# A graph network kernel: the one-hot of a group made in four pieces between the additions of an earlier group

## The reference, cut to what matters

```
score = einsum(leaky_relu(xl[src] + xr[dst] + ee), att)      # edges x 4 heads
ex    = exp(score - segment_max(score, dst)[dst])
alpha = ex / segment_sum(ex, dst)[dst]
out   = segment_sum(alpha[:, :, None] * xl[src], dst)         # 6250 x 128
```

## Time and profile before

| | us |
|---|---|
| median of 3 runs (lowest, highest) | 5126.43 (5126.01, 5128.35) |
| the profiled execution: its own time | 5127.16 |
| its span, first to last instruction | 5125.2 |
| weighted pass, memset of `out` to last addition | 4330.4 to 4972.7 |

### The profile page before, as it was taken

How to read it: one execution, slowest core, us unless ns; L and a number is a source line. 1 busy time by engine, 2 the same in 40 slices (tenths; PEclk the granted TensorE clock), 3 DMA queues, 4 the chain that set the end, 5 groups by cost and what they waited for, 6 DMA issues and landing times. The chain is left out here.

```text
span 5125.2 us, 87712 instructions
## 1 busy us (share of the span) xinstructions
PE 3778.5 (74%) x18006; PEld 2578.7 (50%) x18007; DVE 3333.7 (65%) x9875; ACT 1447.6 (28%) x3473; POOL 2911.9 (57%) x2917
## 2 busy tenths in 40 slices
PE   0377777777678888599779988998988983555563
PEld 0266666666534444355446655555555552444441
DVE  5688888888788888423232244554544446788878
ACT  0255555555444444100000022222222221000012
POOL 1477777777457777777600017777777770333334
PEclk9856656565688888699989985555555555999996
DMA  5577777777433332399666636666666663655530
GB/s 103 146 251 246 251 249 252 250 250 249 160 123 97 97 97 88 77 200 201 136 193 203 203 105 173 176 179 172 178 174 176 177 158 73 163 143 142 143 102 25
DMA packets 1057653, 843.57 MB, mean 165 GB/s; under 512 B 546808, under 2 KB 952812, under 8 KB 1044022
## 3 DMA queue, kind: packets, MB, share of 16 engines
q1 hardware_dynamic: 785634, 597.46, 38.9%
q0 software_dynamic: 98096, 176.73, 13.5%
q10 hardware_dynamic: 173844, 68.53, 5.5%
HBM read 601.34 MB, written 167.28 MB: 150 GB/s over the span
## 5 line engine op out<-in xcount | busy, mean ns | idle before, releaser
L2302 POOL DMA_INDIRECT ring<-xl_rows,idx x896 | 896.4, 1000 | 788.5 <-DVE idx L2381 513.8
L413 POOL DMA_INDIRECT ringa<-x_sign_pos,idxa x880 | 865.0, 983 | 302.1 <-issue 296.0
L965 POOL DMA_INDIRECT edge_counts<-edge_cnt,places x832 | 820.7, 986 | 360.9 <-issue 272.0
L2374 PE MATMUL zps<-We,eaT 64*128 64x128 f32 x1792 | 710.8, 498 | 0.0
L2648 PE MATMUL ops<-val,hot 128*128 128x200 f32 x1792 | 369.7, 351 | 273.8 <-DVE out L2667 244.5
L2372 PE MATMUL zps<-xr,hotT 128*128 x2688 | 454.1, 301 | 149.8 <-ACT hotT L2354 76.6
L2404 DVE TENSOR_TENSOR z<-zps,ring 128x512 f32<-128x512 f32 x224 | 154.9, 691 | 607.8 <-PE zps L2374 505.5
L2374 PEld LDWEIGHTS zps<-We,eaT 64*128 64x128 f32 x1792 | 447.4, 309 | 163.6 <-issue 145.9
L2615 POOL TENSOR_TENSOR val<-rows,val 128x512 f32<-128x512 f32 x224 | 234.4, 1047 | 508.4 <-ACT val L2634 488.4
L498 PE MATMUL sela<-hota,endsa 128*128 128x128 f32 x1760 | 392.7, 393 | 132.3 <-ACT endsa L439 118.2
L2648 PEld LDWEIGHTS ops<-val,hot 128*128 128x128 f32 x1792 | 301.9, 193 | 341.5 <-DVE out L2667 307.8
(11 more groups left out here) (365 smaller groups left out, 5971.9 us busy)
## 6 DMA issues: line engine op xcount, KB each, us to landing
edge_counts<-zeroa SPq DMA_DIRECT2D x55, 1568.0 KB
matd<-edge_counts SPq DMA_DIRECT2D x12, 6272.0 KB
keyb<-edge_keys SPq DMA_DIRECT2D x50, 1216.0 KB
dstb<-dst_in_tile SPq DMA_DIRECT2D x112, 512.0 KB
xl_of_steps<-ring SPq DMA_DIRECT2D x224, 256.0 KB
rows<-xl_of_steps SPq DMA_DIRECT2D x224, 256.0 KB
reseta<-resets SPq DMA_DIRECT2D x110, 512.0 KB
dstba<-dst_in_tile_bf ACTq DMA_DIRECT2D x112, 256.0 KB
```

The costliest lines, as they stand in the source:

```text
L413: p.indirect_dma_start(out=ring[:, k, :], out_offset=None, in_=table, in_offset=bass.IndirectOffsetOnAxis(ap=idx[:, k:k + 1], axis=0)).the ...
L965: p.indirect_dma_start(out=g.M.rearrange("d s -> (d s)").unsqueeze(1), out_offset=bass.IndirectOffsetOnAxis(ap=g.place[:, c:c + 1], axis=0 ...
L2302: p.indirect_dma_start(out=ring[:, c, k, :], out_offset=None, in_=g.xl_rows[0:N, :], in_offset=bass.IndirectOffsetOnAxis(ap=idx[:, q * GS ...
L2374: ins = t.matmul(zk, eaT[:, c, k, :], g.We[:, :], start=False, stop=True)
```

## The change

The one-hot of a group is made by four `tensor_scalar` instructions of 128 columns (comparison of `iota_n` with one column of `drel`) in place of one `tensor_tensor` of 512. The first stands in front of the first addition of group G - 2, the second between the first and the second addition, and so on. The registers for the tiles of group G - 2 are loaded in front of the first piece. `s_hot` counts pieces, and TensorE waits for (G + 1) * GS of them. Each of the four additions has the wait for `s_o`, which the first alone had.

```diff
-                        wait(t, s_hot, G + 1)
+                        wait(t, s_hot, (G + 1) * GS)
...
-                def add(G, q):
+                def tiles_of(G):
                     v.load(regs, g.T[0:1, bass.ds(G * GS, GS)])
-                    T = [v.snap(r, min_val=0, max_val=NT - 1) for r in regs]
+                    return [v.snap(r, min_val=0, max_val=NT - 1) for r in regs]
+
+                def one_hot(G, c, k):
+                    v.tensor_scalar(hot[:, c, k, :], g.iota_n[:, :], g.drel[:, bass.ds(G * GS + k, 1)], None,
+                                    ALU.is_equal).then_inc(s_hot, 1)
+
+                def add(G, q, k, T):
                     wait(v, s_o, G + 1)
-                    for k in range(GS):
-
-                        wait(v, s_out, G * GS + k)
-                        to = g.out[:, bass.ds(T[k] * FX, FX)]
-                        v.tensor_tensor(to, to, ops[q % 2][k // 2][:, (k % 2) * FX:(k % 2 + 1) * FX], ALU.add
-                                        ).then_inc(s_out, 1)
+                    wait(v, s_out, G * GS + k)
+                    to = g.out[:, bass.ds(T[k] * FX, FX)]
+                    v.tensor_tensor(to, to, ops[q % 2][k // 2][:, (k % 2) * FX:(k % 2 + 1) * FX], ALU.add
+                                    ).then_inc(s_out, 1)
 
                 def body(it):
                     for q in range(NG3):
                         G, c = it * NG3 + q, q % NG
+                        adding = not (isinstance(it, int) and q < 2)
+                        if adding:
+                            T = tiles_of(G - 2)
                         wait(v, s_o, G - NG + 1)
-                        v.tensor_tensor(hot[:, c, :, :], bc_mid(g.iota_n[:, :], GS),
-                                        bc_last(g.drel[:, bass.ds(G * GS, GS)], P), ALU.is_equal).then_inc(s_hot, 1)
-                        if not (isinstance(it, int) and q < 2):
-                            add(G - 2, (q - 2) % NG)
+                        for k in range(GS):
+                            one_hot(G, c, k)
+                            if adding:
+                                add(G - 2, (q - 2) % NG, k, T)
                 turns(v, body, TURNS3)
                 for b in (2, 1):
-                    add(TURNS3 * NG3 - b, NG - b)
+                    T = tiles_of(TURNS3 * NG3 - b)
+                    for k in range(GS):
+                        add(TURNS3 * NG3 - b, NG - b, k, T)
```

## The result

The changed kernel takes 5153.04 us, median of 5 runs (5148.91 to 5157.31), beside 5128.35 for the kernel before in the same session: ratio 1.0047, 95% interval 1.0034 to 1.0059. It is slower by 25 us. The forecast was 5239, slower by 112; 5153 lies inside its range of 5121 to 5290, but the likeliest case (5197 to 5294) is refuted. Rival C, at 5155 to 5185, was nearest in number.

What follows compares the result with a forecast made beforehand. ScalarE's full queue was taken to set 2.76 us a group; with GpSimd stopping a piece each turn, 3.29. 212 groups x (3.29 - 2.76) = 112 on top of 5127 gave 5239 us, range 5121 to 5290.

Steps and rivals of the forecast that it cites:

- Rival C: VectorE's pieces are stopped now and then, two regimes alternating; 5155 to 5185 us; chance 0.13.
- the likeliest case: GpSimd's multiplication is tied to VectorE and stops a piece every turn; 5197 to 5294 us; chance 0.60.
- The pacemaker: ScalarE's full queue, with four DMA issues a group, sets 2.76 us a group in the kernel before.
- The elastic stop: On VectorE before the change, the one-hot stands still while GpSimd works; VectorE needs 2.49 of 2.76 us, so nothing is lost.
- The piece is stopped by GpSimd: A VectorE tensor_scalar waits out GpSimd's multiplication, taking 0.8 to 1.1 us and ending within 0.1 of its end.
- The pairs: On VectorE, a piece fits between dependent additions: 0.505 us a pair as before, bounds 0.48 and 0.57; added waits cost nothing.
- Where the multiplication falls: Above 2.69 us a turn, GpSimd's multiplication follows VectorE and stops a piece; the group was taken as 3.29 us.
- before piece 3 and before piece 0 no s fits: With turn 2.52 + s, s the loss per turn, no steady state has GpSimd stopping VectorE's last or first piece.
- x + 0.55: Turn's loss in us when GpSimd's multiplication starts x behind the addition in front of the stopped piece; x 0 to 0.45.
- the tied regime: GpSimd's multiplication, bound to VectorE through TensorE and ScalarE, keeps stopping piece 1 or 2; turns 3.31 or 3.05 us.
- Rival A: GpSimd's multiplication settles in the gap at VectorE's turn head, x 0.1 to 0.2, turn 2.7; 5127 us; chance 0.20.
- Rivals B and D: B: VectorE is the bound, additions' waits get covered, 5082 us, chance 0.02. D: additions leave no gap, 5203, chance 0.02.

Runs made afterwards that it cites:

- one wait: Changed kernel, but only a group's first addition waits for TensorE (s_o); 5127.10 us, ratio 0.9998, on the main chip.
- waits swapped: Changed kernel with an addition's two waits written in the other order, s_out first, then s_o; 5129.79 us, ratio 1.0007.
- one wait, SyncE issues 2: Changed kernel with s_o waited for at the first addition only, and two of a group's four feature DMAs issued by SyncE instead of ScalarE; 5213.53 us, ratio 1.0164.
- before, SyncE issues 2: Kernel before, with two of a group's four feature DMAs issued by SyncE instead of ScalarE; 6546.07 us on another chip, ratio 0.9971.

## Why the prediction was wrong, and where it was right

**The pacemaker: right.** With two DMAs fewer in ScalarE's queue the kernel before runs 2.610 for 2.762. **The elastic stop: right.** Taken away, it changes no time. **The piece is stopped by GpSimd: right**: every stopped piece of the changed kernel ends 0.080 to 0.084 behind the end of the multiplication, within the 0.1 predicted.

**The pairs: 0.505 is right for the pieces, wrong for the waits.** The forecast took 0.20 for a piece and fitted it under the 0.50; it takes 0.28, and the pair is 0.505 all the same, as the next addition starts some 0.06 before the piece is over (4603.10 + 0.28 against 4603.32). The other half of the step failed. The forecast said that the added waits "are for things long done. Nothing." They are what makes the change slower at all. Alone they cost 0.07 in three pairs of six groups in eight, and that counts because of what it uses up. VectorE's undisturbed turn is 0.98 (piece at 0.77 behind the last addition, addition 0.21 behind it) + 3 x 0.505 = 2.49, with 0.20 in hand under ScalarE's 2.69. With three pairs of 0.575 it is 2.70: nothing in hand. (The forecast's upper bound for a pair was 0.57, but for a longer piece and not for the waits; that the two numbers agree is chance.) In the runs without the costly order ScalarE never waits (0.001 a group); in the changed kernel it waits 0.079.

**Where the multiplication falls: the step of the 112 us that failed.** The sum priced a group at 3.29 for 2.76, a loss of 0.53; measured is 2.850, a loss of 0.088. The forecast held that once a turn is over 2.69, a regime with T of 3.05 to 3.31 holds itself, with piece 1 or 2 stopped, and that "before piece 3 and before piece 0 no s fits". Measured over groups 56 to 200: in the changed kernel 84 last pieces and 12 first ones are stopped, none of the second or third. The error is in the price of a stop of the last piece, x + 0.55. It counts the piece's wait but not what the queue does during it: the load of T and its register operations run, and the next first piece starts at 0.27 for 0.77. Half a microsecond comes back, so by the same sum a stop of the last piece costs x + 0.05. The eight turns of a loop pass (last addition to last addition, the median of each over groups 56 to 200) are 2.68, 2.95, 2.65, 3.02, 2.68, 2.32, 2.71 and 3.63 us, a mean of 2.83, and not 3.29. I had used the same overlap for the kernel before (the load runs "behind hot's back") and did not carry it over. That the half microsecond comes back is measured; that it is what keeps the tied regime from holding is argued from the forecast's own sum, and no run takes it away alone. The sum for the tie has a slip too: its terms, 0.42 + 1.62 + 0.15 + 1.97 + 0.33, make 4.49 and not 4.55, which lowers both tied turns by 0.03 and changes nothing here.

**Rival A: right for all but the waits, and given 0.20.** In "one wait" and "waits swapped" the multiplication starts a median of 0.15 and 0.19 behind the last addition (4 in 10 lie between 0.1 and 0.2), and the median turn is 2.67 to 2.68: the numbers of that rival. The 5127 is its number as well. The order of time with the waits swapped:
```profile
4601.70 0.36 DVE L2671 TENSOR_TENSOR out<-out,ops 128x200 f32 x1
4601.78 1.05 POOL L2615 TENSOR_TENSOR val<-rows,val 128x512 f32<-128x512 f32 x1 [1.62 <-ACT val L2634]
...
4602.47 0.44 DVE L2664 TENSOR_SCALAR hot<-iota_n,drel 128x128 f32<-128x128 f32 x1 [0.41 <-issue]
4602.83 0.35 DVE L2671 TENSOR_TENSOR out<-out,ops 128x200 f32 x1
```
The piece is stopped for 0.16 (0.44 for 0.28), at the head, where ScalarE's margin covers it. The argument against this rival, a restart that comes at a bad place, did not weigh: by group 56 the balance has found its place. **Rival C** was near in number only. Its price was a quarter to a half of the tied loss, from turns that alternate with the tied regime; in the trace the long turns (3.63, once in each pass) are those with the loop's turn, and no second or third piece is ever stopped in groups 56 to 200, as the tied regime would have it.

**A regime of the tied length exists**, but in another kernel and by another chain: "one wait, SyncE issues 2", at 3.14 a group. There GpSimd waits mostly for the rows, 222.3 of its 330.1 us idle, where in the kernels at 2.76 it waits for ScalarE alone. The kernels with the same waits of SyncE run at 2.610 without pieces and at 2.652 with pieces that cannot be stopped, so it takes both, a tie through SyncE and stops. That the tie runs through SyncE is argued; no run changes the order of the rows' DMA alone in this kernel.

**Rivals B and D: refuted.** Pairs of 0.505 with a piece of 0.28 between show that an addition's 0.50 has a gap in it which a piece fills. The Trainium skill ("VectorE: DVE Perf Modes", The DRAIN you can't avoid) says that a semaphore after each operation costs nothing extra, and also that a next operation which is not held starts earlier. The trace agrees with the second, 0.28 to the next independent instruction, and not with the first, 0.505 between additions that wait for each other. For the stop, the Trainium skill ("SBUF — State Buffer", Who interferes with whom) names the operands' place, beside the mode, as what decides; the runs agree, 0.28 to 1.05 from SBUF and never over 0.354 with the input in PSUM.

## What to carry to other kernels

When an instruction waits for two things, look at the order in which the queue holds the two waits: the awaited one has to be last. With a wait met long ago behind it, each link of the chain cost 0.07 us more here, and that turned a change worth nothing into a loss of 25 us. And price a stall by what the queue gets done behind it, not by its length; then ask whose margin it eats.

## What the runs showed of the hardware that was not expected

- Two waits of one VectorE instruction are two queue operations, and their order shifts its start by 0.07 us (0.575 against 0.505).
- The stop goes both ways: who begins first keeps its length, and the other waits. In the trace of the changed kernel:
```profile
4517.77 0.28 DVE L2664 TENSOR_SCALAR hot<-iota_n,drel 128x128 f32<-128x128 f32 x1
4517.82 1.14 POOL L2615 TENSOR_TENSOR val<-rows,val 128x512 f32<-128x512 f32 x1 [2.04 <-ACT val L2634]
```
  The piece began 0.047 before the multiplication and kept its 0.28; the multiplication took 1.14 for 1.05. A one-hot of 512 columns that began 0.03 before it made it 1.56 ("before, SyncE issues 2", at 5867.67). Over all runs with pieces that read SBUF, a piece that began 0.047 or more before the multiplication was never stopped, and the 25 that began 0.045 or less before it all were.
- A 128-column comparison with one column operand takes 0.28 from SBUF and 0.347 with its input in PSUM, but the latter is never stopped, and GpSimd's operation keeps its 1.047.
- Taking half of the DMA issues off the queue that sets the pace made "one wait" slower by 86 us (5213.53 against 5127.10) when the pieces could be stopped; when they could not, the kernel was 17 faster than the kernel before (5111.26 against 5128.51).
